# Reloading the values of the next sample by halves, and issuing the first slots and a row after them

## The reference

```python
k, v = ln(ctx) @ wk + bk, ln(ctx) @ wv + bv
slots = q_mu + exp(q_logsig) * layernorm(x)
for _ in range(3):
    q = ln(slots) @ wq + bq
    attn = softmax(k @ q.T * sqrt(512)) + 1e-8        # over the slots
    upd = (attn / attn.sum(tokens)).T @ v
    slots = upd @ wu + bu + slots
    slots = gelu(ln(slots) @ w1 + b1) @ w2 + b2 + slots
    slots = ln(slots + cond)
x1 = x + slots
y = layernorm(x1)                # its rows are scored by w_router; 256 a sample go on
out = x1 + (y, with the block's result in the routed rows)
```

## Time and profile before

| what | value |
|---|---|
| median of three runs | 2549.41 us (2543.11, 2549.41, 2551.65) |
| profiled execution | 2548.73 us |
| its span in the trace | 2547.0 us |
| TensorE busy | 2364.5 us, 93% of the span |
| VectorE, ScalarE, GpSimd busy | 63%, 38%, 41% |
| DMA, mean over the span | 62 GB/s, 158.59 MB |
| mean granted clock of TensorE | 0.968 of full speed |

### The profile page before, as it was taken

The page is one execution under the profiler, slowest core; times in us unless marked ns, Lnnn a source line. Parts: engine busy times, 40 slices in busy tenths (PEclk is TensorE's granted clock), DMA queues, the critical chain, the costliest instruction groups (busy, mean ns, idle before and its releaser), DMA issues. The chain is left out here.

```text
span 2547.0 us, 31016 instructions
## 1 busy us (share of the span) xinstructions
PE 2364.5 (93%) x11492; PEld 1918.5 (75%) x11492; DVE 1603.7 (63%) x2932; ACT 976.0 (38%) x1646; POOL 1056.9 (41%) x1528
## 2 busy tenths in 40 slices
PE   7988799999999999999899999989999987897997
PEld 3776688888877888887788888778888866665786
DVE  5777755747656585767557476755757776644442
ACT  0455423333332433342243333324333335564331
POOL 0455505244271624436263453636345377443200
PEclk9899999999999999999999999999999998998999
DMA  3566200000033000012400001240000121104230
GB/s 120 204 242 242 85 1 1 1 1 1 34 113 144 5 21 5 18 42 106 151 5 21 5 9 50 100 157 5 21 5 9 51 83 50 34 24 118 75 116 17
DMA packets 87782, 158.59 MB, mean 62 GB/s; under 512 B 12233, under 2 KB 34761, under 8 KB 84558
## 3 DMA queue, kind: packets, MB, share of 16 engines
q1 hardware_dynamic: 83238, 150.26, 17.1%
q0 software_dynamic: 2944, 6.31, 0.8%
q10 hardware_dynamic: 1450, 0.04, 0.0%
HBM read 106.21 MB, written 50.38 MB: 61 GB/s over the span
## 5 line engine op out<-in xcount | busy, mean ns | idle before, releaser
L211 PE MATMUL ps<-zTh,kTl 128*128 128x512 f32 (+1 forms) x912 | 336.9, 369 | 26.8 <-ACT prob L1678 22.8
L213 PE MATMUL ps<-zTh,kTh 128*128 128x512 f32 (+1 forms) x912 | 328.4, 360 | 0.0
L212 PE MATMUL ps<-zTl,kTh 128*128 128x512 f32 (+1 forms) x912 | 328.2, 360 | 0.0
L211 PE MATMUL ps<-vh,prob_lo 128*128 128x512 f32 x768 | 307.3, 400 | 11.5 <-DVE prob_lo L2049 11.5
L213 PE MATMUL ps<-vh,prob_hi 128*128 128x512 f32 x768 | 300.2, 391 | 0.0
L212 PE MATMUL ps<-vl,prob_hi 128*128 128x512 f32 x768 | 299.3, 390 | 0.0
L1834 DVE TENSOR_TENSOR zTl<-ps,zTh 128x512 fp32r<-128x512 f32 x224 | 151.1, 684 | 230.7 <-ACT zTh L1559 230.7
L2210 POOL TENSOR_SCALAR rs_m<-mv_m 128x1 f32<-128x1 f32 x96 | 39.6, 412 | 610.4 <-DVE mv_m L1768 608.4
L1678 ACT ACTIVATE prob<-ps,nb 128x1024 f32<-128x1024 f32 x96 | 107.3, 1118 | 298.2 <-DVE nb L2072 298.2
L211 PEld LDWEIGHTS ps<-zTh,kTl 128*128 128x128 f32 x912 | 174.6, 191 | 61.2 <-ACT prob L1678 26.5
L1541 ACT ACTIVATE zbuf<-slots,rs_m 128x512 f32<-128x512 f32 x96 | 78.4, 816 | 344.5 <-POOL rs_m L2214 344.5
(11 more groups left out here) (308 smaller groups left out, 5754.7 us busy)
## 6 DMA issues: line engine op xcount, KB each, us to landing
ctx<-in_ctx_dram SPq DMA_DIRECT2D x8, 1024.0 KB, 11.6
slots<-in_x_dram SPq DMA_DIRECT2D x8, 1024.0 KB, 11.9
kT_d<-kTh SPq DMA_DIRECT2D x6, 1024.0 KB, 4.5
kT_d<-kTl SPq DMA_DIRECT2D x6, 1024.0 KB, 6.8
s_d<-slots SPq DMA_DIRECT2D x6, 1024.0 KB, 4.4
v_d<-vh SPq DMA_DIRECT2D x6, 1024.0 KB, 6.4
v_d<-vl SPq DMA_DIRECT2D x6, 1024.0 KB, 9.3
kTh<-kT_d SPq DMA_DIRECT2D x3, 2048.0 KB, 10.4
```

Of the source, the lines that this page charges most:

```text
L211: nc.tensor.matmul(out, ll, rh, start=start, stop=False)
L212: nc.tensor.matmul(out, lh, rl, start=False, stop=False)
L213: return nc.tensor.matmul(out, lh, rh, start=False, stop=stop)
```

## The change

On the SyncE queue the two loads of the values (2 MB each) become four of 1 MB, each for four tiles. `load_values(k, half)` loads tiles 4*half to 4*half+3 of `v[k]`. The first half of `vl` is issued when ScalarE has read the first four tiles of `aux`, the first half of `vh` when the first half of `stg` has landed in `x1_d`, and the second halves likewise. The load of the finished sample's first tile (`finish_in`) now stands behind the issue of the second write, and not behind its landing. The loads into `slots` and `cb_row` come after all of these. TensorE waits for four landings of values in place of two. On GpSimd the addition for tile 3 is moved up to that for tile 2.

```diff
@@ SyncE, at a change of sample @@
                 sp.dma_start(kT[1][:, :, :].bitcast(f32), kT_d[b + 1, 1]).then_inc(sem("kT_in"), 16)
-                for k in range(2):
+
+                def load_values(k, half):
+                    sp.dma_start(v[k][:, cut(half, 4), :].bitcast(f32), v_d[b + 1, k, :, cut(half, 4), :])\
+                        .then_inc(sem("v_in"), 16)
+
+                def result_out(k):
                     sp.wait_ge(sem("x1_ready"), b * NT + 4 * k + 4)
                     sp.dma_start(four(x1_d[b * S + k * 512:b * S + (k + 1) * 512, :]), stg[:, cut(k, 4), :])\
                         .then_inc(sem(f"x1_out{k}"), 16)
+
+
+                sp.wait_ge(sem("zo_z"), n8 + NT + 4)
+                load_values(1, 0)
+                result_out(0)
+                sp.wait_ge(sem("x1_out0"), (b + 1) * 16)
+                load_values(0, 0)
+                sp.wait_ge(sem("zo_z"), n8 + 2 * NT)
+                load_values(1, 1)
+                result_out(1)
+                finish_in(b, 0, 0, g + 1)
+                sp.wait_ge(sem("x1_out1"), (b + 1) * 16)
+                load_values(0, 1)
+                for k in range(2):
                     sp.dma_start(slots[:, cut(k, 4), :], four(s0_d[b + 1, cut(k, 512), :]))\
                         .then_inc(sem(f"s0s_in{k}"), 16)
                 sp.wait_ge(sem("cb_added"), n8 + NT)
                 sp.dma_start(cb_row[:, :], cb_d[b + 1].partition_broadcast(P)).then_inc(sem("cb_in"), 16)
-                for k in range(2):
-                    sp.wait_ge(sem(f"x1_out{k}"), (b + 1) * 16)
-                finish_in(b, 0, 0, g + 1)
-                sp.dma_start(v[0][:, :, :].bitcast(f32), v_d[b + 1, 0]).then_inc(sem("v_in"), 16)
-                sp.wait_ge(sem("zo_z"), n8 + 2 * NT)
-                sp.dma_start(v[1][:, :, :].bitcast(f32), v_d[b + 1, 1]).then_inc(sem("v_in"), 16)
@@ TensorE, ahead of the update @@
                 if t == 0 and b:
-                    pe.wait_ge(sem("v_in"), b * 2 * 16)
+                    pe.wait_ge(sem("v_in"), b * 4 * 16)
@@ GpSimd, end of a round @@
-                x1(2)
+                x1(2, 3)
                 rstd_z(5); rstd_p(7)
                 rstd_z(6); rstd_z(7)
-                x1(3, 4, 5, 6, 7)
+                x1(4, 5, 6, 7)
```

## The result

| | before | changed kernel |
|---|---|---|
| median | 2548.47 us (4 runs, 2543.11 to 2551.65) | 2532.11 us (4 runs, 2526.72 to 2532.84) |
| ratio | | 0.9933, 95% interval 0.9911 to 0.9955 |
| profiled execution, span | 2548.73, 2547.0 us | 2526.72, 2525.0 us |

The account below looks back on a forecast made before the run. TensorE, busy 93% of the span, was taken to lose time only by idling or half clock, led by three waits. 20.6 + 7.6 - 1.5 - 3.8 - 1.6 - 1.8 = 19.5 us less gave 2529 us, range 2519 to 2542.

Parts of the forecast that it names:

- The chain and the cure: At each change of sample, tbuf's landing holds VectorE, ScalarE, then TensorE; issuing tbuf behind the second write removes 20.6 us.
- The leftover at tbuf: Waiting for prob that stays ahead of tile 4's logits: 0.5 us at each change of sample, 1.5 us in all.
- X: Issue time of the second write of the results at each change of sample; 765.53 at the first.
- The half clock behind the waits: TensorE's matmuls run at half clock after each of the three waits; full clock returns, 7.6 us less.
- x1(3): On GpSimd, tile 3's addition ahead of tile 5's scale delays TensorE 1.28 us per change of sample: 3.8 us added.
- The clock behind that wait: After TensorE's wait for the normalised tile 5, the clock falls in one of three places: 1.6 us added.
- Idle time at the update's start: TensorE waits for VectorE's prob_lo as the update begins: 0.6 us each, 1.8 us in all.
- Rival A: zbuf lands at X + 27, holding TensorE's tile 7 for 4.1 us per change: 2549, half-way 2539; chance 0.13.
- My bound: Latest landing of zbuf that TensorE's tile 7 of the logits can bear without waiting: X + 22.9.
- B: Transfers drain so slowly that tbuf lands at X + 10.5; waits stay, 2548 to 2549; chance 0.12 with half-way landings.
- C: Value reads mixed with a write slow the second write; tbuf lands at X + 17: 2568 us; chance 0.05.

Follow-up runs that it names:

- the run with the writes first: Changed kernel with GpSimd's order of before, both writes then tbuf issued ahead of the value halves except vl's first half: 2534.70 us, ratio 0.9944.
- The best kernel: The run with the writes first, plus GpSimd's x1(0) moved behind tile 3's scale and zbuf loaded right behind tbuf: 2518.76 us, ratio 0.9877.

## Why the prediction was right, point by point

- **The chain and the cure.** Right. The three waits (20.6 us) are gone; what is left for prob is 0.3 us or less each time. That tbuf's landing set them is shown by moving it alone, one way (2539) and the other (2574).
- **The leftover at tbuf, 1.5 us.** It was 0. Mis-sized. I took 6.1 to 6.4 us for the second write; in the changed kernel it landed in 5.5, 4.8 and 5.0 us, and tbuf 6.2, 5.4 and 5.6 us behind X, where I had 6.9 to 7.3. The two halves ahead of it had been issued 7.7 and 4.1 us before, and had probably drained for the most part; how far is not measured. What stands ahead decides: the run with GpSimd as before shows 10.8 to 13.9 us for the same write behind two halves issued 0.8 and 0.5 us before. The formula of the Trainium skill ("DMA: Bandwidth & Descriptors", section "Anatomy of one DMA — SWDGE (gpsimd) path"), which is given for GpSimd's path, makes 4.4 us of a 1 MB transfer. The first writes of the changed kernel (4.3 us), with nothing issued shortly before them, agree with it; the second ones (4.8 to 5.5) lie above it, and the 10.8 to 13.9 us far above.
- **The half clock behind the waits, 7.6 us.** Right: no slow matmul stands between 767.30 and the update, nor at the same place of the other two changes; the granted clock of these three stretches is 1.00.
- **x1(3), 3.8 us.** The place was right, the size too small: (2.14 - 0.36) x 3 = 5.3 us. 0.5 us of each come on top of the addition's 1.28, and they lie in the small instructions of the scale (2.06 us from first to last, where one addition alone stood ahead they took 1.5). VectorE's instruction at 748.14 lies beside GpSimd's additions and takes 1.72 us in place of 0.73.
- **The clock behind that wait, 1.6 us.** Mis-sized: I took one place of three, and it was all three, about 1.6 us each, 4.8 in all. The idle time was 2.14 us and not the 1.64 that I weighed. It is partly chance: with tbuf late, the same idle time was followed by the half clock in one place of three, with only GpSimd's part in two. My comparison of 1.50 us (full clock) with 1.82 us (half clock) did not hold even in the trace before. At the second change an idle time of 1.49 us, 2.5 us behind one of 1.39, is followed by the half clock, and an idle time of 1.82 us at 1167.41 is not:

```profile
1184.72 0.80 PE L211 MATMUL ps<-w2h,gT1l 128*128 128x512 f32 x1 [1.49 <-POOL gT1l L2310]
1185.32 0.63 PE L212 MATMUL ps<-w2l,gT1h 128*128 128x512 f32 x1
```

- **Idle time at the update's start, 1.8 us.** It was 0 in the changed kernel. Idle time does appear there (1.5 to 3.0 us) when zbuf is late, but by way of zbuf and not of the spared waits from which I had reckoned it.
- **Sum.** 20.6 + 7.6 - 5.3 - 4.8 = 18.1 us by the terms as they came, 19.0 between the marks of the three changes, 16.4 by the medians (22.1 in the later comparison), 19.5 forecast. Two terms were too pessimistic by 1.5 and 1.8 us, two too optimistic by 1.5 and 3.2. That they nearly cancelled is luck; the mechanism is not.
- **Rival A, zbuf takes tbuf's place.** Its mechanism did not occur in the changed kernel: zbuf landed at X + 17.7, X + 20.9 and X + 20.7 (I had 19 to 20), and VectorE waited 0.2 us for it, once. But it decides the neighbours: by the medians 13.4 us hang on it with both writes and tbuf ahead of the values. My bound (TensorE's tile 7, X + 22.9, or X + 21.6 without the 1.28 us of x1(3)) held roughly: in the run with the writes first zbuf landed at X + 21.6, X + 24.1 and X + 26.0, and tile 7 waited 0, 1.80 and 3.64 us. What I left out is a tighter deadline behind it, the start of the update, which waits for VectorE's split: it waited 2.08 us in the first place, where tile 7 waited for nothing.
- **Rivals B and C.** The changed kernel is in neither; the run with GpSimd as before (10.8 to 13.9 us for the second write, 2553) is. So that mechanism was real, and x1(3) keeps the kernel out of it. The run with tbuf late (2574) is another thing: its second write landed within 5.5 us, and tbuf was late because it stood behind the slots and the row.

What the halves do in the changed kernel: they let 3 MB of values be issued before tbuf, most of it long before. That splitting gives nothing by itself is shown for the order with tbuf and zbuf ahead of the values, where whole loads are as fast; whole loads at the changed kernel's own places were not tried. The best kernel is 7.4 us below the changed one in the same comparison (2518.76 and 2526.20). What x1(3) costs, 5.3 + 4.8 = 10.1 us, less tbuf's wait that is partly back, would be of that size, but this is argued and not shown: it was not tried by itself, and x1(0) differs as well.

## What to carry to other kernels

Where one queue serves all transfers, look for the small load that an in-order engine waits for, and put it ahead of the large ones that nobody needs yet; splitting the large ones is only a way to get them out of its path. When such a wait is taken away, follow the next small load in the queue, and reckon every later deadline that hangs on it (here the start of the update as well as the next tile), and not only the first that comes to mind. A step that is moved up on an engine without a pause is paid with more than its own duration if TensorE's idle time behind it grows to where the clock falls.

## What the runs showed of the hardware

Two things were not expected. A 1 MB write to DRAM, the second one of a change, took from 4.8 us (changed kernel) to 13.9 us (GpSimd as before) to land in the same place of the program, by what had been issued just before it. And a VectorE instruction of 0.73 us took 1.72 us, three times of three in the changed kernel, where two GpSimd additions of 128x512 ran back to back and it began beside the second (748.14, above). With one addition, ended before it began, it took 0.73. The other traces say more of it. Wherever such an instruction (SCALAR_TENSOR_TENSOR, 128x512, all its operands in the on-chip memory) lay beside one of these additions, 27 times in nine traces, it took about 0.55 us plus the time that it lay beside: 1.71 to 1.73 us with 1.17 beside, 1.56 with 1.0, 1.12 with 0.57. That is as if it did its work only behind the addition. VectorE's BATCH_NORM_STATS2, and its TENSOR_TENSOR with an input in PSUM, kept their 0.69 us beside the same additions. Why they differ was not tried.
